# Two mixture-of-experts stages list their tokens by an inverting matmul and gather them block by block

## The reference

```python
out = _swiglu(flat, shared_gate, shared_up, shared_down)     # DFF = 512
probs = jax.nn.softmax(flat @ router_w.T, axis=-1)           # E_ROUTED = 7
top_vals, top_idx = jax.lax.top_k(probs, 2)
top_vals = top_vals / (top_vals.sum(-1, keepdims=True) + 1e-09)
combine = jnp.sum(jax.nn.one_hot(top_idx, E_ROUTED) * top_vals[..., None], axis=1)
for e in range(E_ROUTED):
    routed = routed + combine[:, e:e+1] * _swiglu(flat, routed_gate[e], routed_up[e], routed_down[e])
return out + routed
```

## Time and profile before

| | us |
|---|---|
| median of 3 runs | 1266.48 |
| lowest, highest | 1263.84, 1274.41 |
| the profiled execution, first to last instruction | 1288.7 |

### The profile page before, as it was taken

How to read it: one execution, slowest core, us unless ns; L and a number is a source line. 1 busy time by engine, 2 the same in 40 slices (tenths; PEclk the granted TensorE clock), 3 DMA queues, 4 the chain that set the end, 5 groups by cost and what they waited for, 6 DMA issues and landing times. The chain is left out here.

```text
span 1288.7 us, 30057 instructions
## 1 busy us (share of the span) xinstructions
PE 1028.3 (80%) x12227; PEld 718.2 (56%) x12237; DVE 841.0 (65%) x1508; ACT 525.7 (41%) x1329; POOL 574.0 (45%) x393
## 2 busy tenths in 40 slices
PE   6538877887889999998365798899497999957895
PEld 2127666666774555555265355655377455533795
DVE  5469999999896775567322787487322788855233
ACT  2534444444443742552132274175144577502121
POOL 3389999999964613101435310110524321002232
PEclk9859999999899999999588899899689899978898
DMA  2198899998875000000473000000465000003792
GB/s 114 45 226 213 233 232 230 224 223 228 211 224 190 2 1 1 1 2 1 114 205 110 20 2 1 1 1 2 162 183 192 1 2 2 1 1 95 254 305 83
DMA packets 74376, 139.77 MB, mean 108 GB/s; under 512 B 8144, under 2 KB 28384, under 8 KB 73888
## 3 DMA queue, kind: packets, MB, share of 16 engines
q1 hardware_dynamic: 70272, 129.67, 36.0%
q0 software_dynamic: 3968, 8.18, 1.8%
HBM read 128.06 MB, written 14.82 MB: 111 GB/s over the span
## 5 line engine op out<-in xcount | busy, mean ns | idle before, releaser
L888 ACT ACTIVATE shifted_a<-scores,nmax_a 128x128 f32<-128x128 f32 x768 | 208.6, 389 | 77.4 <-DVE nmax_a L832 75.9
L1445 ACT ACTIVATE decay<-decay 128x1016 f32<-128x1016 f32 x128 | 124.0, 1002 | 152.5 <-PE decay L1331 152.4
L832 DVE TENSOR_REDUCE nmax_a<-scores 128x4 f32<-128x512 f32 x192 | 123.6, 686 | 69.6 <-PE scores L718 67.4
L364 POOL TENSOR_TENSOR rstd<-ve,neghalf 128x4 f32<-128x4 f32 x30 | 31.5, 1051 | 255.9 <-DVE ve L349 255.9
L1331 PE MATMUL decay<-delta,A_pairs 32*128 32x127 f32 x2048 | 83.3, 300 | 75.4 <-DVE small_pack L1489 34.0
L1785 POOL DMA_INDIRECT results<-xs_s x76 | 72.9, 960 | 120.9 <-DVE xs_s L1960 114.5
L838 DVE COPY PTs_a<-PT 128x512 f32<-128x512 f32 x192 | 123.1, 682 | 2.6 <-PE PT L728 2.6
L1331 PEld LDWEIGHTS decay<-delta,A_pairs 32*128 32x128 f32 x2048 | 69.7, 201 | 94.9 <-DVE small_pack L1489 39.4
L728 PE MATMUL PT<-mamba_pack,shifted_a 128*128 128x128 f32 x768 | 106.3, 280 | 4.4 <-DVE PTs_a L838 2.6
L728 PEld LDWEIGHTS PT<-mamba_pack,shifted_a 128*128 128x128 f32 x768 | 82.3, 141 | 30.3 <-issue 19.2
L1303 POOL TENSOR_TENSOR pos_bias<-pos_bias,B 128x1024 f32<-128x1024 f32 x36 | 85.4, 2407 | 1.9 <-DMA pos_bias<-du_rows 1.9
(11 more groups left out here) (482 smaller groups left out, 2272.5 us busy)
## 6 DMA issues: line engine op xcount, KB each, us to landing
pos_bias<-du_rows SPq DMA_DIRECT2D x72, 256.0 KB, 5.2
small_pack<-L3f_w SPq DMA_DIRECT2D x15, 768.0 KB
XN<-du_rows SPq DMA_DIRECT2D x38, 256.0 KB, 5.0
XNT<-du_rows SPq DMA_DIRECT2D x38, 256.0 KB, 5.0
O<-du_rows SPq DMA_DIRECT2D x36, 256.0 KB, 5.0
masked_cos<-du_rows SPq DMA_DIRECT2D x36, 256.0 KB, 5.0
masked_sin<-du_rows SPq DMA_DIRECT2D x36, 256.0 KB, 5.3
small_pack<-L2f_w SPq DMA_DIRECT2D x15, 514.0 KB
```

What stands on the lines that cost most here:

```text
L364: nc.gpsimd.tensor_tensor(rstd[:, bs], ve[:, bs], m.neghalf[:, bs], ALU.pow).then_inc(m.rstd_ready, 1)
L832: nc.vector.tensor_reduce(nmax[:, u % 4, :], scores[u % 4], AX.X, ALU.min).then_inc(m.maxed, 1)
L888: t = nc.scalar.activation(shifted[u % 4][:, j, :], scores[u % 4][:, j, :], ACT.Exp, scale=-1.0, bias=nmax[:, u % 4, j:j + 1])
L1445: nc.scalar.activation(x, x, ACT.Exp).then_inc(decayed, 1)
```

## The change

Layer 1 keeps its scatters; layers 2 and 3 (`GATHERED`) lose them, the copies, the reload and the fourteen matmuls. In their place:

- SyncE stores all tokens to a DRAM array `tokens`.
- `Listing` inverts the slot list. VectorE splits each slot into block and place (`split`) and writes two one-hot arrays in bf16, sixteen compares for the places. ScalarE and GpSimd scale the other one by token number, batch and choice. Sixteen matmuls (`invert`) give, for each slot, its token; an empty slot gets token 0. VectorE turns that into two lists of rows (`number`), where to read from and where to return to.
- GpSimd gathers each block's 128 rows from `tokens` by one indirect DMA: the first AHEAD = LAG + 8 blocks in front of the loop, block j + AHEAD right behind the store of block j.
- The first group has one block, the second three.
- The weights are applied in `combine`, in all three layers: sixteen operations of one batch in place of four of half the batches. `weigh` becomes a plain copy, `copy_y`.
- Layer 3: four shared units stand before the rank matmuls, the gates of the shared expert move to GpSimd, fed by copies that ScalarE makes.
- Layer 2: the context products move in front of the rank matmuls, with the bias added by a matmul of one row, copied by ScalarE; the transforms follow the rank matmuls.
- Semaphores left from the first stage are used again, and two of three start-up fills of slot arrays go.

```diff
+class Listing:
+    def split(self, dve, slot, steps):
+        steps.done(dve, nc.vector.tensor_scalar(self.ahead[:], slot[:], -63.75, 1.0 / 128.0, ALU.add, ALU.mult))
+        steps.done(dve, nc.vector.tensor_scalar(self.ahead[:], self.ahead[:], ROUND, None, ALU.add))
+        steps.done(dve, nc.vector.tensor_scalar(self.block_of[:], self.ahead[:], -ROUND, None, ALU.add))
+        nc.vector.tensor_tensor(self.in_block[:], bcast_mid(m.w("iota128")[:, 0:n], 16), bcast_last(self.block_of[:], n),
+                                ALU.is_equal).then_inc(self.blocks_known.sem, self.blocks_known.by(1))
...
+        for g in range(16):
+            t = nc.vector.tensor_scalar(self.at_place[:, g, :], self.iotab[:], self.place_in[:, g:g + 1], None,
+                                        ALU.is_equal)
+            if g % 4 == 3:
+                t.then_inc(self.places_known.sem, self.places_known.by(1))
+    def invert(self, pe):
+        pe.wait_ge(self.lows_scaled.sem, self.lows_scaled.at(1))
+        pe.wait_ge(self.batches_scaled.sem, self.batches_scaled.at(1))
+        for g in range(16):
+            if g % 4 == 0:
+                pe.wait_ge(self.places_known.sem, self.places_known.at(g // 4 + 1))
+            t = self.nc.tensor.matmul(self.ps, self.at_place[:, g, :], self.scaled[:, g, :, :].rearrange("p x j -> p (x j)"),
+                                      start=(g == 0), stop=(g == 15))
+        t.then_inc(self.inverted.sem, self.inverted.by(1))
...
+    if DIRECT:
+        GROUPS = [range(0, 1), range(1, 4)] + GROUPS[1:]
+    next_group = {js[min(1, len(js) - 1)]: q + 1 for q, js in enumerate(GROUPS[:-1])}
+    AHEAD = min(DIRECT, LAG + 8)
...
         @block.gpsimd
+            def gather(j):
+                done = gathered[j % GATHERS]
+                if j >= GATHERS:
+                    pool.wait_ge(done.sem, done.at(16 * (j // GATHERS)))
+                nc.gpsimd.indirect_dma_start(xs[:, j, 0:D], None, m.dram["tokens"],
+                                             bass.IndirectOffsetOnAxis(ap=listing.source_i[:, j:j + 1], axis=0)
+                                             ).then_inc(done.sem, done.by(16))
...
+                for j in range(AHEAD):
+                    gather(j)
...
             for j in range(NB):
-                pool.wait_ge(y_weighed.sem, y_weighed.at(j + 1))
-                number = xs[:, j, D:D + 1].bitcast(I32)
+                pool.wait_ge(y_copied.sem, y_copied.at(j + 1))
+                number = listing.result_i[:, j:j + 1] if j < DIRECT else xs[:, j, D:D + 1].bitcast(I32)
                 nc.gpsimd.indirect_dma_start(results, bass.IndirectOffsetOnAxis(ap=number, axis=0), xs[:, j, 0:D], None
                                              ).then_inc(returned.sem, returned.by(16))
+                if j + AHEAD < DIRECT:
+                    gather(j + AHEAD)
...
             def turn(q):
-                pe.wait_ge(slots_loaded[q].sem, slots_loaded[q].at(16))
+                if q in slots_loaded:
+                    pe.wait_ge(slots_loaded[q].sem, slots_loaded[q].at(16))
...
                 for j in GROUPS[q]:
+                    if j < DIRECT:
+                        done = gathered[j % GATHERS]
+                        pe.wait_ge(done.sem, done.at(16 * (j // GATHERS + 1)))
...
             if gated:
                 pe.wait_ge(shared_loaded.sem, shared_loaded.at(16))
-                for u in range(UPS):
+                for u in range(4):
                     shared_up(u)
+            if transforms:
+                pe.wait_ge(ones_set.sem, ones_set.at(1))
+                context.products(pe)
             pe.wait_ge(steps.sem, route.onehot_value)
...
         def combine(dve, half):
             dve.wait_ge(brought[half].sem, brought[half].at(32))
-            steps.done(dve, nc.vector.tensor_tensor(x, x, back[:, 0, halves[half], :], ALU.add))
-            nc.vector.tensor_tensor(x, x, back[:, 1, halves[half], :], ALU.add).then_inc(combined.sem, combined.by(1))
+            for k in range(2):
+                for b in range(halves[half].start, halves[half].stop):
+                    t = nc.vector.scalar_tensor_tensor(out=m.X[:, b, :], in0=back[:, k, b, :],
+                                                       scalar=route.wt[:, b, k:k + 1], in1=m.X[:, b, :],
+                                                       op0=ALU.mult, op1=ALU.add)
```

More of the change, by code:

```diff
@@ L36 @@
 PAIRS, QUADS = 64, 16
-ROW = D + 2
+ROW = D + 1
 BLOCKS = {"L1f": 31, "L2f": 23, "L3f": 22}
+GATHERED = {"L1f": 0, "L2f": 23, "L3f": 22}
+SCATTERED = [layer for layer in BLOCKS if GATHERED[layer] < BLOCKS[layer]]
+ROUND = 1.5 * 2.0 ** 23
 class Steps:
@@ L1292, in _ @@
                          ).then_inc(m.bias_loaded, 16)
-            for layer in ("L1f", "L2f", "L3f"):
+            for layer in SCATTERED:
                 slots = m.dram[f"slots_{layer}"]
@@ L1698, in sparse_stage @@
             shared_hid = [m.pos_bias[:].rearrange("p (c x) s -> p c (x s)", c=FC), sb("shared_hid", [128, FC, HALF])[:]]
-            shared_loaded, shared_down = sem("shared_loaded"), sem("shared_down")
+            shared_loaded, shared_up_done, shared_taken, shared_gated, shared_down = (
+                sem(f"shared_{n}") for n in ("loaded", "up_done", "taken", "gated", "down"))
+            shared_units = [(half, fc) for half in range(2) for fc in range(FC)]
         else:
@@ L1852, in _ @@
             nc.tensor.matmul(rank[:, N:2 * N], m.not_earlierb[:], chosen, start=True, stop=True).then_inc(ranked.sem, ranked.by(1))
+            if transforms:
+                context.transform(pe)
             if gated:
[L1854 removed]
+                for u in range(4, len(shared_units)):
                     shared_up(u)
+                if DIRECT:
+                    listing.invert(pe)
                 for half in range(2):
@@ L1871, in _ @@
                 pe.wait_ge(begun.sem, begun.at(2))
-                if context is not None:
-                    context.products(pe)
-                    context.wait_copied(pe)
-                pe.wait_ge(scattered.sem, scattered.at(16 * 12))
-            for i in range(0 if gated else 14):
-                nc.tensor.matmul(Y[1][:], m.identb[:], m.q_mask[:, 0:4 * S], start=True, stop=True)
+                if DIRECT < NB:
+                    pe.wait_ge(scattered.sem, scattered.at(16 * 12))
+                    for i in range(14):
+                        nc.tensor.matmul(Y[1][:], m.identb[:], m.q_mask[:, 0:4 * S], start=True, stop=True)
             turn(0)
@@ L1880, in _ @@
                 up(j)
-                if j % 4 == 1 and j // 4 + 1 < len(GROUPS):
-                    turn(j // 4 + 1)
+                if j in next_group:
+                    turn(next_group[j])
                 if j >= LAG:
@@ L1903, in _ @@
                                          ).then_inc(comb_copied.sem, comb_copied.by(1))
-                if context is not None:
-                    context.copy(act)
                 for j in range(NB):
@@ L1967, in begin @@
                 nc.vector.tensor_tensor(x, x, four(source[half]), ALU.add).then_inc(begun.sem, begun.by(1))
-            if gated:
-                for u in range(2 * FC):
-                    gate(u, shared_hid[u // FC][:, u % FC, :])
-                for half in range(2):
-                    begin(half, shared_down)
-            else:
+            if not gated:
                 oh = onehot[:].rearrange("p e (k b) -> p k b e", k=2)
@@ L1979, in _ @@
                 nc.vector.tensor_tensor(comb[:], comb[:], part[:], ALU.add).then_inc(comb_ready.sem, comb_ready.by(1))
-                if residual is not None:
-                    dve.wait_ge(residual_added.sem, residual_added.at(1))
-                begin(0, b2_done)
-                begin(1, b2_done)
-            if context is not None:
-                context.add_bias(dve)
+            if DIRECT:
+                listing.number(dve, steps)
+            if residual is not None:
+                dve.wait_ge(residual_added.sem, residual_added.at(1))
+            for half in range(2):
+                begin(half, shared_down if gated else b2_done)
             copy_turned(0)
```

283 lines of the change are left out of this document (203 added, 80 removed).

## The result

| | before | after |
|---|---|---|
| plain runs, median (us) | 1267.9 (1263.84 to 1274.41, 4 runs) | 1325.75 (1324.38 to 1327.66, 4 runs) |
| profiled span | 1288.7 | 1324.7 |

The changed kernel is **slower**: 1.0455 times the time before, 95% interval 1.0424 to 1.0486, some 58 us. The forecast was 1276.4, the range 1262 to 1291: right in sign, far too small.

What follows compares the result with a forecast made beforehand. TensorE was taken to bound the block loop, with a lead-in ahead of it. Lead-ins -12.3 and -12.4, loops +13.2 and +16.8, sums +4.6 made +9.9: 1276.4 us, range 1262 to 1291.

Steps and rivals of the forecast that it cites:

- the bound 0.08: Layer 3 lead-in, VectorE's 128x128 bf16 compares: lower bound in us for one compare; 0.2 was taken.
- The estimate of 0.1: VectorE's bf16 compares near 0.1 us each; layer 2's loop would start 1.6 us and layer 3's 0.5 earlier.
- The sums: End of all three stages: sixteen weighted 128x128 adds replace four of 128x512, plus 4.6 us.
- At 0.117 they take 7.5, at the low clock 0.236 ... 15.1: rank at 914.0 to 921.6.: Layer 2 lead-in: 64 context and bias matmuls ahead of rank take 7.5 to 15.1 us; rank taken at 917.
- The clock: Layer 2's loop start: TensorE might begin at granted clock 0.50, costing 1.7 us beyond the other waits.
- Landing 2.0.: Block loops: a gather lands 2.0 us after issue; stalls 11.1 us in layer 3, 12.0 in layer 2.
- the bound 3.65: Layer 3's loop: upper landing time in us, from the last scatter behind a weight burst; 4.9 us more.
- Three things ride along at nothing.: Layer 3 lead-in: gates on GpSimd, SyncE's store of tokens and VectorE's wait for the inverted list cost nothing.
- Rival 2: Lead-ins: late matmul updates belong to profiling (7 more, 1284) or to the weight burst (about 6 more, 1283); 25%.
- Rival 3: Loops: weights, stores and gathers fill the DMA, every landing 3.65 us; 4.9 and 6.6 more, 1288; 13%.
- rival 1: GpSimd's queue behind the copies: turns find their rows, stalls of 11.1 and 12.0 us go, 1253.3; 7%.

Runs made afterwards that it cites:

- the two runs on the bias: Changed kernel with the context's bias added by VectorE, 1305.09 us; changed kernel with the one-row bias products behind all context products, 1312.52 us.
- the fill: Changed kernel with fourteen idle matmuls ahead of each TensorE turn that waits for a gather behind a store: 1316.35 us, ratio 1.0353.
- The second profile: The kernel before, unchanged, profiled again: time 1268.27 us, span 1266.5.

## Why the prediction was too low

**Right.** A gather stands behind a store, TensorE's turn waits for it, copies come in fours: the mechanism and its places. Eight weighted adds take 2.31, as forecast; but the first up matmul came 12 us sooner in neither stage. The sixteen compares take 3.24 in layer 2, 0.20 each in the mean, as taken, which is part luck: two of them, beside GpSimd's products for the list, take 0.44 each, the other fourteen 2.35 together, 0.17 each (the bound 0.08 no run shows). The estimate of 0.1 from the Trainium skill (VectorE: DVE Perf Modes, The perf-mode tier table, with the cost table of its section The TRN2 errata) is not borne out by them. From rank to the first up matmul in layer 2 it took 16.5 us, 17 forecast. The sums cost 5.2, 4.6 forecast.

**Wrong**, with what each step is short of the measured 58.2 - 9.9 = 48.3:

- *"At 0.117 they take 7.5, at the low clock 0.236 ... 15.1: rank at 914.0 to 921.6."* The 64 instructions took 23.1, above the upper end; 10.5 had been taken. The bounds came from rows of like instructions in a row; none alternates one row with 128. Shown by the two runs on the bias. **12.6.**
- *The clock.* The sum holds 1.7 for a low clock at layer 2's start and nothing behind the waits that the same sum puts into TensorE's queue. The slow matmuls behind them cost 4.9 us in layer 2 and 4.7 in layer 3; the fill shows it, in all three such turns of layer 2 and in two of three in layer 3. **9.6.**
- *"Landing 2.0."* From the end of its issue to its turn a group's last gather took 2.5 to 5.2 us in the seven waits, 3.6 in the mean: the bound 3.65 was the value. It had been set aside because a waiting TensorE would let the weight queue run dry; the weights of the blocks just freed were still coming (the DMA engines were 0.45 to 0.98 busy in layer 2's stalls). Stalls 16.1 and 15.3 us in place of 12.0 and 11.1. **8.3.**
- *"Three things ride along at nothing."* Two did not. The gates held up VectorE (rank to the first gather's issue 16.0 us, 11.3 forecast). TensorE did not wait for that gather in layer 3; it waited for the compares, so the shared down products began 13.0 us after rank and not 8.7. This is shown. And the store of the tokens ran beside the shared weights that TensorE waited for, with the first shared units at the low clock behind that (rank 2.4 late). Half of this is shown by the four runs that move the store: the first shared matmul comes 4.7 to 5.1 us after the router's products in them, 5.3 to 5.9 in the kernels that don't, 4.6 to 4.8 before. The other half, the low clock, went in two of the four and stayed in two. **7.1.**
- *The base.* Rival 2 priced at 7 that the waits on late matmuls belong to the one profile of before, 25%. The second profile bears it out: the lead-ins are 6.1 shorter in layer 2 and 1.1 in layer 3. **7.2.**

Sums 2.1 and rest 1.4. Each of these terms missed in the same direction, so the range, made of single misses, held none of it. Rival 3 (landings of 3.65) was right on the landing and gave 1288, since it priced nothing behind it; rival 1 (turns that find their rows) is the run with all gathers first, and its 23 us for the stalls became 40 there, with the clock. Not settled: how large the sums' part is (the stretch behind layer 1's loop took 208.0 to 213.5 us in profiles with weighted adds, 202.1 to 206.2 with wide ones), some 2 us between layer 2's last copy and layer 3's router that stay with the wide adds (180.9 against 179.0), and why a landing in the loop takes 3.6 us, where the last store before had 1.3: in the last 2.0 us of the wait that ends at 1248.95 the DMA engines are only 0.27 busy.

## What to carry over

A wait put into TensorE's queue cost its length and then, in six of seven turns here, the clock: price both. Work that depends on nothing in a loop, like these gathers, belongs ahead of it, not on a queue behind the loop's own results. "Moved to an idle engine" was not free where the two engines held each other up, and a sum should rest on two profiles of the kernel before, or on one whose span agrees with the plain runs.

## What the runs showed of the hardware

- One-row products in turns with 128-row ones: 0.36 us per instruction and a granted clock of 0.50 in a stretch in which TensorE was busy 23.10 of 23.10 us; in two blocks 0.17 and 0.12 us, and the clock rises.
- A GpSimd product of two 128x512 SBUF operands (1.27 us) stretches a VectorE step of 0.17 us to 1.25, until it ends.
- The first gather of layer 3, issued into the burst of weights, is used 5.8 to 6.2 us after the end of its issue in the five kernels in which TensorE waits for it, with gather and weights on different queues.
- A 128x128 compare in bf16 with a scalar per row took 0.17 us of VectorE's timeline, 0.44 beside GpSimd's products.
- Two profiles of one kernel differed by 22 us of span, 18 of them in one loop.
